# State-space passes: where the C rows are split, who weighs the states, and the order of Silu and convolution

## The reference, cut to what matters

```python
def mamba(x, in_w, conv_w, conv_b, xproj_w, dt_w, dt_b, Alog, Dp, out_w):
    xs, z = jnp.split(jnp.einsum('bld,ed->ble', x, in_w), 2, axis=-1)   # 256 channels each
    xs = silu(conv1d(xs, conv_w, 4 taps) + conv_b)
    dt, Bc, Cc = jnp.split(jnp.einsum('bld,ed->ble', xs, xproj_w), [8, 24], axis=-1)
    dt = jax.nn.softplus(jnp.einsum('blr,dr->bld', dt, dt_w) + dt_b)
    dA = jnp.exp(dt[..., None] * -jnp.exp(Alog))                        # 16 states
    dBx = dt[..., None] * Bc[:, :, None, :] * xs[..., None]
    # per token: h = dA_t * h + dBx_t ; y = einsum('bds,bs->bd', h, C_t)
    y = (ys + Dp * xs) * silu(z)
    return jnp.einsum('bld,od->blo', y, out_w)
```

## Time and profile before

| | us |
|---|---|
| median of 3 runs | 7933.69 (7930.62 to 7936.44) |
| the profiled execution | 7936.57 |
| its span, first to last instruction | 7934.7 |
| TensorE busy over the span | 6766.5 (85%) |
| VectorE busy | 5401.0 (68%) |
| ScalarE busy | 3986.9 (50%) |
| GpSimd busy | 2874.4 (36%) |

### The profile page before, as it was taken

One profiled execution on the slowest core, in us unless ns is written; L12 is line 12 of the kernel. 1 busy time (PEld: TensorE's weight loads), 2 busy tenths in 40 slices (PEclk: granted clock), 3 DMA queues, 4 the chain that ended last, 5 costly groups with the idle time before them and its releaser, 6 DMA issues. The chain is left out here.

```text
span 7934.7 us, 189955 instructions
## 1 busy us (share of the span) xinstructions
PE 6766.5 (85%) x74958; PEld 4244.1 (53%) x75040; DVE 5401.0 (68%) x8827; ACT 3986.9 (50%) x6001; POOL 2874.4 (36%) x1663
## 2 busy tenths in 40 slices
PE   7989993887696788887888868989989999989998
PEld 5766682443342333333333325667657666667676
DVE  7876465554546888886888873658757777767544
ACT  4555333554444566655555564545534444446433
POOL 3311263232214777766777740126302222211000
PEclk9999996988888888988888879999999999999999
DMA  0000001000001111111111100000000000000000
GB/s 26 0 19 12 2 0 17 3 3 2 9 1 51 63 64 63 64 48 68 62 64 64 64 33 12 13 10 0 3 27 2 2 2 2 2 11 14 15 0 21
DMA packets 95823, 186.39 MB, mean 23 GB/s; under 512 B 20502, under 2 KB 54749, under 8 KB 94845
## 3 DMA queue, kind: packets, MB, share of 16 engines
q1 hardware_dynamic: 95356, 179.82, 7.1%
HBM read 172.36 MB, written 5.31 MB: 22 GB/s over the span
## 5 line engine op out<-in xcount | busy, mean ns | idle before, releaser
L2443 POOL TENSOR_TENSOR m_dBx<-m_dtx,m_Bs 128x1024 f32<-128x1024 f32 x518 | 1213.7, 2357 | 504.0 <-DVE m_hs L2762 462.9
L2762 DVE TENSOR_TENSOR_SCAN m_hs<-m_ps_dA,m_dBx 128x512 f32<-128x512 f32 x1036 | 1208.6, 1208 | 172.5 <-ACT m_ps_dA L2644 84.3
L2554 PE MATMUL m_ps_y<-m_yc,ident 128*128 128x512 f32 x2072 | 1097.1, 656 | 55.4 <-DVE m_yc L2770 50.4
L2644 ACT ACTIVATE m_ps_dA<-m_dt,m_A 128x504 f32<-128x504 f32 x1036 | 683.4, 678 | 501.4 <-DVE m_hs L2762 491.9
L2770 DVE TENSOR_TENSOR m_yc<-m_hs,m_ps_C 128x1024 f32<-128x1024 f32 x518 | 623.5, 1204 | 97.0 <-PE m_ps_C L2537 71.9
L1998 POOL TENSOR_TENSOR a_s<-a_s,a_den 128x1024 f32<-128x1024 f32 x128 | 243.5, 1902 | 1151.9 <-DVE a_den L2044 1151.9
L2554 PEld LDWEIGHTS m_ps_y<-m_yc,ident 128*128 128x128 f32 x2072 | 438.7, 213 | 394.6 <-issue 368.8
L2537 PE MATMUL m_ps_C<-m_parts,m_sel 128*128 128x512 bf16 x438 | 186.4, 426 | 332.3 <-DVE m_yc L2770 329.8
L2537 PEld LDWEIGHTS m_ps_C<-m_parts,m_sel 128*128 128x128 bf16 x520 | 51.5, 99 | 652.5 <-DVE m_yc L2770 568.1
L580 POOL TENSOR_TENSOR c_kbd<-c_kf,c_hmask 128x1024 f32<-128x1024 f32 x66 | 124.9, 1893 | 526.7 <-ACT c_kf L493 513.8
L2042 DVE TENSOR_REDUCE a_den<-a_s 128x16 f32<-128x1024 f32 x128 | 156.0, 1219 | 208.3 <-ACT a_s L1950 208.3
(11 more groups left out here) (745 smaller groups left out, 16455.8 us busy)
## 6 DMA issues: line engine op xcount, KB each, us to landing
m_Bs<-m_B_rows SPq DMA_DIRECT2D x260, 512.0 KB, 3.6
c_kvb<-in_ctxT SPq DMA_DIRECT2D x68, 128.0 KB, 2.1
c_kvb<-in_ctxT SPq DMA_DIRECT2D x17, 256.0 KB, 2.7
out_dram<-X SPq DMA_DIRECT2D x1, 4096.0 KB
m_B_rows<-m_low SPq DMA_DIRECT2D x34, 32.0 KB, 3.1
c_table<-in_table SPq DMA_DIRECT2D x2, 512.0 KB
x_xr<-X SPq DMA_DIRECT2D x8, 128.0 KB, 4.6
x_pT<-in_ctx SPq DMA_DIRECT2D x8, 128.0 KB
```

What stands on the lines that cost most here:

```text
L2443: return nc.gpsimd.tensor_tensor(to, one, other, ALU.mult)
L2554: last = nc.tensor.matmul(ps_y[:, m, :], C.ident[:], yc[:, s % 2, m, :], start=s == 0, stop=s == NS - 1)
L2644: nc.scalar.activation(seqs(ps_dA[:, h % 3, :]), seqs(dt[:, par, m, :]), ACT.Exp, scale=A[:, m, s:s + 1]).then_inc(decay, 1)
L2762: nc.vector.tensor_tensor_scan(hs[:, s % HS, m, :], ps_dA[:, (2 * s + m) % 3, :], dBx[:, s % BX, m, :], 0.0, ALU.mult, ALU.add).then_inc(s ...
```

## The change

- Two weighings of each group, of states 4 and 9, go from VectorE to GpSimd (`weigh` there, ahead of its products for states 8 and 13). They are made in place in `hs`, with a C row that SyncE loads from DRAM spread over the partitions (`Cs`). TensorE sums these two from `hs`, and VectorE's scan four states later waits for that sum. TensorE spreads 14 C rows instead of 16.
- B and C rows (32) are stored; the 16 C rows come back as 128x64 (`piece`), VectorE splits them in five operations (`split_rows`, after its weighing 7), the three bf16 parts are stored and loaded as 48 rows of `parts`. ScalarE's copy of the high part and VectorE's four old operations are gone. The low products are made on 64 rows, into `ps_k`.
- The four Silu evaluations stand alone, each with its own return to the other table: after ScalarE's states 0 and 3 (convolution), 11 and 14 (gate). Low rows are copied at s = 5, and the softplus steps stand one state later.
- TensorE: low products at s = 2, convolution at 12, 13, 14 and its last step at s = 0 of the turn after; project writes to `ps_j`.
- `dtx` has one buffer; GpSimd drains once more before it is written.

```diff
     nc = C.nc
     AHEAD = 3
     SLOTS, CHUNK, BX, HS = 4, 2, 4, 4
+    POOL_WEIGHS = (4, 9)
+    DVE_WEIGHS = [s for s in range(NS) if s not in POOL_WEIGHS]
+    NDW, NPW = len(DVE_WEIGHS), len(POOL_WEIGHS)
+    SKIPPED, SPLIT, PIECE = 6, 8, NS * GT // P
     FREE_HALVES, FREE_STATES, FREE_ROWS = 3, SLOTS * CHUNK, 1
...
+            def store_rows(j, par):
+                sp.wait_ge(rows_low, j + 1)
+                sp.dma_start(BC_rows[par], low[0:2 * NS, :]).then_inc(rows_stored, 16)
+                sp.wait_ge(rows_stored, j * 16 + 16)
                 sp.sem_inc(begun, 1)
+                sp.dma_start(piece[:], BC_rows[par, NS:2 * NS, :].rearrange("s (q t) -> (s q) t", t=PIECE)).then_inc(piece_loaded, 16)
+
+            def load_parts(j, par):
+                sp.wait_ge(split_ready, j + 1)
+                sp.dma_start(part_rows[par].rearrange("k (p t) -> p k t", t=PIECE), split[:]).then_inc(split_stored, 16)
+                sp.wait_ge(split_stored, j * 16 + 16)
+                sp.sem_inc(begun, 1)
+                sp.dma_start(parts[0:3 * NS, par, :], part_rows[par].rearrange("k (s t) -> (k s) t", t=GT)).then_inc(parts_loaded, 16)
 
             def spread_B(j, par, c):
 
                 sp.wait_ge(dBx_ready, j * NS + CHUNK * c + CHUNK)
-                rows_ = B_rows[par, CHUNK * c:CHUNK * c + CHUNK, :]
+                rows_ = BC_rows[par, CHUNK * c:CHUNK * c + CHUNK, :]
                 sp.dma_start(Bs[:, c % SLOTS, :, :], bc(rows_.unsqueeze(0), [P, CHUNK, GT])).then_inc(B_loaded[c % SLOTS], 16)
+
+            def spread_Cs(j, par):
+                sp.wait_ge(hs_weighed, j * NPW + NPW)
+                for k, s in enumerate(POOL_WEIGHS):
+                    sp.dma_start(Cs[:, k, :], bc(BC_rows[par, NS + s:NS + s + 1, :], [P, GT])).then_inc(Cs_loaded, 16)
 
             with sp.Fori(0, C.NG // 2) as pair:
                 for par in range(2):
-                    store_B(pair * 2 + par, par)
+                    store_rows(pair * 2 + par, par)
                     for c in range(NS // CHUNK):
+                        if c == 2:
+                            load_parts(pair * 2 + par, par)
+                        if c == 3:
+                            spread_Cs(pair * 2 + par, par)
                         spread_B(pair * 2 + par, par, c)
-            store_B(C.NG, 0)
...
                 hold()
-                multiply(dBx[:, s % BX, :, :], dtx[:, par, :, :],
+                multiply(dBx[:, s % BX, :, :], dtx[:],
                          bc(Bs[:, slot, s % CHUNK, :].unsqueeze(1), both)).then_inc(dBx_ready, 1)
+
+            def weigh(j, s):
+
+                k = POOL_WEIGHS.index(s)
+                pool.wait_ge(scanned, j * (2 * NS) + (2 * s + NHF + FREE_HALVES))
+                pool.wait_ge(Cs_loaded, j * (16 * NPW) + 16 * NPW)
+                hold()
+                multiply(hs[:, s % HS, :, :], hs[:, s % HS, :, :], bc(Cs[:, k, :].unsqueeze(1), both)).then_inc(hs_weighed, 1)
 
             def front(j, s, par):
...
-                    multiply(dtx[:, par, :, :], dt[:, par, :, :], xs[:, par, :, :])
+                    pool.drain()
+                    multiply(dtx[:], dt[:, par, :, :], xs[:, par, :, :])
                     pool.drain()
 
...
                     for s in range(AHEAD, NS):
+                        if s - BX in POOL_WEIGHS:
+                            weigh(i, s - BX)
...
-            def convolve(j, m, step):
+            def convolve(j, m, step, behind=True):
 
                 if m == 0 and step == 0:
                     pe.wait_ge(hT_ready, j + 1)
+                if m == 1 and step == 0 and behind:
+                    pe.wait_ge(z_ready, j * NHF)
...
                 for m in range(NHF):
-                    last = nc.tensor.matmul(ps_j[:], xp[:, m, :], xs[:, par, m, :], start=m == 0, stop=m == NHF - 1)
+                    last = nc.tensor.matmul(ps_k[0:64, :], xp[:, m, :], xs[:, par, m, :], start=m == 0, stop=m == NHF - 1)
                 last.then_inc(dbl_done, 1)
 
             def step_sizes(j, in_loop):
-                pe.wait_ge(parts_ready, j + 1)
+                pe.wait_ge(rows_low, j + 1)
                 if in_loop:
...
                 last.then_inc(dt_done, 1)
 
-            def spread_C(s, par):
-                nc.tensor.matmul(ps_C[:], sel[:, s, :], parts[:, par, :], start=True, stop=True).then_inc(C_done, 1)
+            def spread_C(j, s, par):
+                if s == 0:
...
@@ -2542,21 +2582,38 @@
 
             def project(i):
                 pe.wait_ge(y_ready, i + 2)
-                pe.wait_ge(xs_ready, i * NHF + 6)
+                pe.wait_ge(xs_ready, i * NHF + 5)
                 for p in range(TPG):
                     for m in range(NHF):
...
 
-            def add_state(s):
+            def add(of, s):
                 for m in range(NHF):
-                    last = nc.tensor.matmul(ps_y[:, m, :], C.ident[:], yc[:, s % 2, m, :], start=s == 0, stop=s == NS - 1)
+                    last = nc.tensor.matmul(ps_y[:, m, :], C.ident[:], of[:, m, :], start=s == 0, stop=s == NS - 1)
                 last.then_inc(y_added, 1)
 
+            def step(j, s, par, between=None):
+                if s in POOL_WEIGHS:
+                    pe.wait_ge(hs_weighed, j * NPW + (POOL_WEIGHS.index(s) + 1 + NPW))
+                    add(hs[:, s % HS, :, :], s)
+                    return
+                rank = DVE_WEIGHS.index(s)
+                pe.wait_ge(yc_ready, j * NDW + (rank + 1 + FREE_ROWS))
+                if rank + 1 < NDW:
+                    spread_C(j, DVE_WEIGHS[rank + 1], par)
+                else:
+                    spread_C(j + 1, 0, 1 - par)
+                if between is not None:
+                    between()
+                add(yc[:, rank % 2, :, :], s)
+
             def front(j, s, par, in_loop):
 
-                if s == 1:
+                if s == 0:
+                    convolve(j, 1, 1)
+                elif s == 2:
                     low_products(j, par)
                 elif s == 4:
...
                     gate(j, 0)
                     gate(j, 1)
                 elif s == 10:
-                    pe.wait_ge(z_ready, j * NHF + 2)
+                    pe.wait_ge(z_ready, j * NHF + 1)
                     turn(j + 1)
-                elif 11 <= s < 15:
-                    convolve(j + 1, (s - 11) // 2, (s - 11) % 2)
+                elif 12 <= s < 15:
...
 
-            def activate(j, par, in_loop):
-
-                if in_loop:
-                    act.wait_ge(y_added, j * NS - 2 * NS + 7)
-                for m in range(NHF):
-                    act.wait_ge(xs_done, j * NHF + m + 1)
-                    nc.scalar.activation(xs[:, par, m, :], bank[m][:], ACT.Silu,
-                                         bias=conv_b[:, m:m + 1]).then_inc(xs_ready, 1)
+            def activate(j, m, par, in_loop):
+
+                if m == 0 and in_loop:
+                    act.wait_ge(y_added, j * NS - 2 * NS + (SKIPPED + 1))
+                act.wait_ge(xs_done, j * NHF + m + 1)
+                nc.scalar.activation(xs[:, par, m, :], bank[m][:], ACT.Silu, bias=conv_b[:, m:m + 1]).then_inc(xs_ready, 1)
+                exponentials()
+
+            def gate(j, m, par, in_loop):
+
+                if m == 0 and in_loop:
+                    act.wait_ge(y_ready, j)
+                act.wait_ge(z_done, j * NHF + m + 1)
+                nc.scalar.activation(sz[:, par, m, :], bank[m][:], ACT.Silu).then_inc(z_ready, 1)
+                exponentials()
 
             def front(j, s, par, in_loop):
-                if s == 3:
-                    act.wait_ge(dbl_done, j + 1)
-                    if in_loop:
-                        act.wait_ge(B_stored, j * 16)
-                    nc.scalar.activation(low[0:64, :], ps_j[0:64, :], ACT.Copy).then_inc(B_low, 1)
-                    nc.scalar.activation(parts[:, par, :], ps_j[:], ACT.Copy).then_inc(high_ready, 1)
+                if s == 0:
+                    activate(j, 0, par, in_loop)
+                elif s == 3:
+                    activate(j, 1, par, in_loop)
                 elif s == 4 and in_loop:
                     act.wait_ge(xT_done, j + 1)
                     normalise(j + 1)
-                elif s == 6:
+                elif s == 5:
+                    act.wait_ge(dbl_done, j + 1)
+                    if in_loop:
+                        act.wait_ge(rows_stored, j * 16)
+                    nc.scalar.activation(low[0:64, :], ps_k[0:64, :], ACT.Copy).then_inc(rows_low, 1)
+                elif s == 7:
                     act.wait_ge(dt_done, j + 1)
                     for m in range(NHF):
                         nc.scalar.activation(e[:, m, :], bank[m][:], ACT.Abs, bias=dt_b[:, m:m + 1])
-                elif s == 7:
+                elif s == 8:
                     act.drain()
                     for m in range(NHF):
                         last = nc.scalar.activation(x[:, m, :], bank[m][:], ACT.Relu, bias=dt_b[:, m:m + 1])
```

(57 more changed lines are left out.)

97 lines of the change are left out of this document (47 added, 50 removed).

## The result

| | before | after |
|---|---|---|
| median, runs of the comparison | 7932.15 us (7926.77 to 7936.44) | 7737.75 us (7729.9 to 7758.19) |
| the profiled execution | 7936.57 | 7758.19 |
| its span | 7934.7 | 7756.4 |
| TensorE, VectorE, ScalarE, GpSimd busy | 6766.5, 5401.0, 3986.9, 2874.4 | 6754.0, 5283.2, 4161.9, 3021.8 |

The ratio is 0.976 (95% interval 0.9744 to 0.9776): 2.4% faster, 194 us by the medians, 178 us between the two profiled executions. The forecast was 7807 us, a gain of 127, with a range from 7740.

A forecast was written before the change was run, and what follows sets the result against it. VectorE was nearest to bounding the kernel, GpSimd would be the new bound. Period 32.8 + 26.5 + 3.15 = 62.5 against 66.6 us, −132 over 32 groups, +5 for prologues: 7810, less 2.9 for the median, 7807 us; range 7740 to 7945.

The forecast's parts named there:

- GpSimd as the new bound: GpSimd's run behind the logarithm: next scan 0 starts 32.8 us after scan 7's end, 4.3 later than VectorE alone.
- The scans 0 to 7: VectorE from scan 0's start to scan 7's end: 26.5 us of work plus 3.15 of stalls per group.
- the loop's edge: VectorE's stop at the loop's turn, once in two groups: 4.7/2 = 2.35 us per group, taken to stay.
- longer prologues: Ahead of the two passes: a four-DMA chain and more table loads add 0 to 10 us, 5 taken.
- the loop's edge and TensorE stalls: Bound on these VectorE stalls: −1 to +1.5 us per group, −32 to +48 us in all.
- The split: VectorE's five C-row operations on 128x64 cost 1.3 to 2.0 us, 1.5 taken, so −1.4 per group.
- rival A: Split operations wait out GpSimd products: one or two caught and covered, or all five, 7990 us; chance 0.13.
- C for states 6 and 7: TensorE's spreads behind GpSimd's weighing of state 4: ready at 7.0 and 10.6 us, wanted at 9.0 and 12.4.
- rival B: TensorE's clock stays at half, C for state 6 comes 3.4 us late: 7916 us, chance 0.14.
- ScalarE and the DMA part: Single-Silu blocks of 3.2 us just fit between exponentials; added loads and stores are costed at zero.
- Rival D: Folded C-row chain through DRAM is late, delaying state 0's spread; over 15 us slack; chance 0.05 with others.
- Rival C: GpSimd's lateness does not tell, period VectorE's 55.0 plus stalls 3.15: 7670 us, chance 0.08.

The follow-up runs named there:

- e_bestlate: Changed kernel with all 16 weighings on VectorE and the split on GpSimd after state 9, logarithm kept at the change's later states: 7698.28 us, ratio 0.9696.
- e_w35: Changed kernel with GpSimd weighing states 3 and 5 instead of 4 and 9: 7770.32 us, ratio 0.9785 to the kernel before.
- e_early: Changed kernel with ScalarE's Relu, Exp, Ln and reciprocal steps one state earlier, as before the change: 7787.75 us, ratio 0.9807.
- e_split12: Changed kernel with VectorE's split after weighing 11 instead of 7, inside GpSimd's unbroken run: 7961.29 us, ratio 1.0031.

## Why the prediction was right, and where it fell short

**GpSimd as the new bound: right, and to size.** Scan 7 ended at 3044.73 + 2.33 = 3047.06. The logarithm, the row

```profile
3051.35 1.06 ACT L2737 ACTIVATE m_ln<-m_v 128x1024 f32<-128x1024 f32 x1
```

ended 5.35 us later (5.5 forecast); the run was 24.9 (25.0); scan 0 of the next group started at 3079.96, 32.9 us after scan 7's end (32.8). In all groups of the loop in which the split isn't caught the run is 24.9 us. The late logarithm put back (e_bestlate) cost 80 us, and taking the weighings off GpSimd gained 18 despite the work that VectorE took over.

**The scans 0 to 7: 26.5 right, the stalls wrong.** From scan 0's start to scan 7's end 3047.06 − 3020.28 = 26.8 us, against 26.5 + 3.15. *This is the step that failed.* The term is the loop's edge, 2.35 us a group, which the forecast wrote down as "once in two groups" and carried over whole. It was read from the first pass alone; in the second pass of the kernel before the stop is 2.5 to 2.8 us. And it doesn't come with every loop: it comes and goes with the loading of code at the backward branch, and in the changed kernel, whose VectorE code is another, the first pass loads none. There a group without a caught cast lasts 59.7 us, which is 32.9 + 26.8. In the second pass every other group still stops, but shorter:

```profile
3647.78 2.34 DVE L2823 TENSOR_TENSOR_SCAN m_hs<-m_ps_dA,m_dBx 128x512 f32<-128x512 f32 x2 [1.90 <-ACT m_ps_dA L2691]
```

The seven stops there are 1.8 to 2.9 us long, 1.0 us a group in the mean. But after each of them the split, being later, has its last cast caught as well, and the two together make such a group 63.4 to 65.5 us long, where others last mostly 59.7: some 2.4 us a group. So in the second pass the term of 2.35 came out nearly right, by luck: half of it is another wait. In the first pass it was 2.35 × 16 = 38 us too much.

The periods say the same: 60.2 is 2.3 us under the 62.5 forecast, 62.1 is 0.4 under it; 37 + 6 us more than the 132, together 175, is what was measured (176). Of the 5 us for longer prologues nothing is seen.

My bound for "the loop's edge and TensorE stalls", −1 us a group, was too narrow: a stop whose cause I had named without showing deserved its whole size as a bound, 75 us in place of 32, and 7738 would have lain inside the range. Which position of a loop avoids the loading I didn't work out; it stays open.

**The split: 1.32 us against 1.5**, inside its bounds. Of rival A the weak form came, as the forecast had it: the last cast, line 2810, is the one that meets GpSimd's run. Line 2804 is beside it for comparison:

```profile
L2804 DVE TENSOR_TENSOR m_rest<-m_piece,m_split x34: 224/226/227, 2462.1 to 4477.3; 128x64 f32<-128x64 f32 x34
...
L2810 DVE CAST m_split<-m_rest x34: 195/195/2390, 2462.9 to 4478.1; 128x64 bf16<-128x64 f32 x34
```

It was caught in 12 of 34, 3 in the first pass and 9 in the second, for 2.2 us each; 7 of the 9 follow a stop at the loop's edge. The reading that the split lies at the end of GpSimd's gap was right, and there is nothing to spare: in the group shown the last cast and GpSimd's first product both start at 3052.58. That such a wait is covered by GpSimd's lateness was wrong. A first-pass group with a caught cast shows why:

```profile
2870.33 2.39 DVE L2810 CAST m_split<-m_rest 128x64 bf16<-128x64 f32 x1
```

```profile
2876.84 2.35 POOL L2499 TENSOR_TENSOR m_v<-m_v,m_e 128x1024 f32<-128x1024 f32 x1 [1.86 <-ACT m_r L2741]
```

The scans behind the cast come later, ScalarE's exponentials and its step `m_r` with them, and GpSimd waits 1.86 us for that in the midst of its run, which is 26.7 to 26.8 us long in all 12 such groups. In the first pass these groups last 61.5 to 62.8 us in place of 59.7. How close it is shows in e_w35, e_early and e_split12 too: each shift of GpSimd's work or of the split lost more than it had promised.

**TensorE: the place right, the state wrong, the price nil.** C for states 6 and 7 was in time as worked out. C for state 11 was not: VectorE stood 3.14 us. The chain is the one in the forecast (TensorE stands for the weighing of state 9, its clock falls, the sum is slow), found at the later weighing:

```profile
3062.35 3.78 PE L2594 MATMUL m_ps_y<-m_hs,ident 128*128 128x512 f32 x4 [3.77 <-POOL m_hs L2468]
3065.93 1.06 PE L2537 MATMUL m_ps_j<-ident,m_xn 128*128 128x128 f32 x4
3066.92 0.60 PE L2577 MATMUL m_ps_C<-m_parts,m_sel 48*128 48x512 bf16 x1
```

The sum took 3.78 us, where 1.88 stood in the earlier trace rows, at a granted clock of 0.51 between 3061.0 and 3067.9, half of 2.4 GHz, after TensorE had been idle for 3.77. This is rival B in another place. It costs nothing by itself because GpSimd is late by more: its run from 3052.58 to 3079.8 does not wait for it, and where the C wait is 0.7 us shorter, scan 0 waits for GpSimd 0.9 us longer. The step sizes of state 4 ran at full clock (1.12 us for a half, as the faster of the two in the earlier trace rows), so rival B did not come where I had put it.

**ScalarE and the DMA part: right.** The wait for exponentials, without the stops at the loop's edge, fell from 21.2 us to 2.4 in some 600 us. The loads and stores of the folded form landed 1.7 to 2.9 us after their issue and held nothing up in the loop (ahead of it VectorE waits some 22 us a pass for the first `piece`, yet the first gate starts at 2543.6 us, before the change at 2550.1); the DMA share rose from 0.18 to 0.24 (2480 to 3520). Rival D didn't come. Rival C didn't either: the lateness of GpSimd does tell, 3.9 us of waits against 4.3 forecast.

**The gain by its causes**, then: the second pass, which stops in both kernels, gained 4.3 us a group and the first 6.7. The 2.4 between them, 38 us over 16 groups, go with the stops that the first pass lost by the position of the code; 64 idle instructions gave the first pass of the kernel before 31 us in the same way. The other 138 us are VectorE's shorter queue and ScalarE's earlier exponentials, less GpSimd's lateness, where 132 were forecast. How they divide between the queue and the exponentials no run shows: none put the folded split or the four Silu blocks alone into the kernel before.
